# Second attention of a four-layer kernel: global keys laid out as a diagonal, scaling on ScalarE, later counts, global values in two parts

## What is computed

```python
s_loc = jnp.einsum('blhd,blwhd->bhlw', Q, Kw) * scale
a_loc = jax.nn.softmax(s_loc, axis=-1)
local = jnp.einsum('bhlw,blwhd->blhd', a_loc, Vw)
Kg = K[:, global_indices]
Vg = V[:, global_indices]
s_g = jnp.einsum('blhd,bghd->bhlg', Q, Kg) * scale
a_g = jax.nn.softmax(s_g, axis=-1)
glob = jnp.einsum('bhlg,bghd->blhd', a_g, Vg)
out = 0.7 * local + 0.3 * glob
x = layernorm(x + (out.reshape(Bb, Ll, Dm) @ Wo.T + bo))
```

## Time and profile before

| what | us |
|---|---|
| median of 3 runs | 1109.08 (1107.51 to 1109.56) |
| the profiled execution | 1103.31 |
| its span, first to last instruction | 1101.6 |
| PE busy | 953.2 (87%) |
| DVE busy | 781.5 (71%) |
| POOL busy | 678.9 (62%) |
| ACT busy | 577.6 (52%) |

### The profile page before, as it was taken

How to read it: one execution, slowest core, us unless ns; L and a number is a source line. 1 busy time by engine, 2 the same in 40 slices (tenths; PEclk the granted TensorE clock), 3 DMA queues, 4 the chain that set the end, 5 groups by cost and what they waited for, 6 DMA issues and landing times.

```text
span 1101.6 us, 27734 instructions
## 1 busy us (share of the span) xinstructions
PE 953.2 (87%) x7536; PEld 699.0 (63%) x7536; DVE 781.5 (71%) x3615; ACT 577.6 (52%) x1250; POOL 678.9 (62%) x1491
## 2 busy tenths in 40 slices
PE   3999999999959995799999999999999319999940
PEld 1777777777735552677777777777776218777830
DVE  3788888888825776457786877777775327888846
ACT  2566676666621332255555555555545007777734
POOL 3566666666631322266769888887879523777765
PEclk9899999999978998599999999999989559999975
DMA  6121111211042441111112121212211166777717
GB/s 184 27 52 32 45 45 31 48 27 45 23 132 91 161 164 80 32 47 34 47 29 59 39 59 48 68 44 60 53 32 38 44 173 234 238 234 250 254 58 212
DMA packets 71375, 98.34 MB, mean 89 GB/s; under 512 B 13688, under 2 KB 43256, under 8 KB 71104
## 3 DMA queue, kind: packets, MB, share of 16 engines
q1 hardware_dynamic: 61040, 83.31, 25.9%
q0 software_dynamic: 4992, 10.30, 2.8%
q10 hardware_dynamic: 5232, 3.42, 1.2%
HBM read 49.48 MB, written 24.77 MB: 67 GB/s over the span
## 4 chain that ended last, share of the span: by engine, by line
PE 73%; DVE 10%; issue 5%; DMA 3%; POOL 3%; ACT 2%; SPq 2%; DVEq 0%; ACTq 0%; POOLq 0%
PE bank L342 6%; PE bank L172 5%; PE bank L253 5%; PE bank L351 4%; PE bank L372 4%; PE bank L1491 4%; PE bank L1492 4%; PE bank L1257 4%; PE bank L1493 4%; PE bank L406 4%; PE bank L168 3%; PE bank L413 3%; PE bank L346 3%; PE bank L381 3%; PE bank L398 2%
## 5 line engine op out<-in xcount | busy, mean ns | idle before, releaser
L528 ACT ACTIVATE p<-bank 128x480 f32<-128x480 f32 (+1 forms) x448 | 240.5, 540 | 247.8 <-PE bank L372 88.0
L663 DVE CUSTOM_DVE_ANT_0 bank<-bank,band 128x160 f32<-128x160 f32 x512 | 156.9, 347 | 82.0 <-PE bank L342 79.5
L663 DVE CUSTOM_DVE_ANT_0 bank<-bank,causal 128x128 f32<-128x128 f32 (+1 forms) x512 | 169.4, 386 | 56.1 <-PE bank L346 40.3
L893 POOL TENSOR_SCALAR_AFFINE_SELECT p<-p 128x380 f32<-128x380 f32 (+1 forms) x256 | 146.5, 602 | 57.2 <-ACT p L528 56.2
L1669 POOL DMA_INDIRECT y_rows<-p,rows x92 | 105.9, 1151 | 67.5 <-DVE p L1622 46.2
L663 DVE DVE_READ_ACCUMULATOR2_ANT nm<- 128x1 f32 x1024 | 143.6, 140 | 0.1
L874 POOL TENSOR_SCALAR_AFFINE_SELECT p<-p 128x256 f32<-128x256 f32 (+1 forms) x192 | 91.0, 486 | 68.3 <-ACT p L528 64.6
L342 PE MATMUL bank<-ks,qs 128*128 128x186 f32 x512 | 118.6, 316 | 3.5 <-issue 2.3
L342 PEld LDWEIGHTS bank<-ks,qs 128*128 128x128 f32 x512 | 81.5, 198 | 38.2 <-issue 23.3
L372 PE MATMUL bank<-qs,ks 128*128 128x160 f32 x512 | 102.2, 303 | 0.0
L1562 ACT ACTIVATE p<-bank,wb 128x512 f32<-128x512 f32 x92 | 63.6, 691 | 39.5 <-PE bank L1493 37.6
(11 more groups left out here) (207 smaller groups left out, 2330.0 us busy)
## 6 DMA issues: line engine op xcount, KB each, us to landing
qs<-parts SPq DMA_DIRECT2D x46, 512.0 KB, 5.2
qs<-qf SPq DMA_DIRECT2D x128, 128.0 KB, 2.4
rows<-xr SPq DMA_DIRECT2D x23, 260.0 KB, 3.7
parts<-ks SPq DMA_DIRECT2D x8, 512.0 KB, 2.8
xs<-x_b SPq DMA_DIRECT2D x16, 256.0 KB, 4.0
p<-in_w SPq DMA_DIRECT2D x12, 256.0 KB, 3.4
xin<-in_x SPq DMA_DIRECT2D x16, 128.0 KB, 2.2
parts<-qf SPq DMA_DIRECT2D x4, 512.0 KB, 2.7
```

The source lines that it names most:

```text
L528: act.activation(pb[:, :, :].rearrange("p u c -> p (u c)")[:, lo:lo + cols], bank[:, 0:cols], ACT.Exp, scale=SCALE).then_inc(L.exp_done, 1)
L663: return dve.tensor_tensor_reduce(at, at, mask, -1.0, -BIG, ALU.add, ALU.min, nm[:, item:item + 1])
L893: pool.affine_select(out=at, in_=at, compare_op=ALU.is_ge, fill=0.0, base=base, pattern=[[0, 4], [sign, hi - lo]], channel_multiplier=-sig ...
```

## The change

- The global keys are laid out by DVE as a diagonal (`lay_out_kg`, 128 x 400 elements, at (1,2)): one full-width matmul for each four heads takes the place of four narrow ones, so that unit 3 exists in quarters 2 and 3 alone, with two f32r matmuls of 256 columns and one exponential over 512 columns each. They read the unspread queries, kept in three buffers (`T.qf`), to which SP sends the maxima's rows as well.
- The global values are multiplied by `global_values` in two parts, at (3,1) and at (0,1), with the exponentials as the stationary operand: four f32 matmuls of 64 columns each, straight into the turned form that `normalise` reads. Part 2 of `pv`, `round_og` and the copy L479 are gone.
- Scaling (`layernorm`) of the local attention is done by ACT at the end of the body; POOL makes the shift for it with two more small operations.
- `round_rp` and `round_rt` stand at (1,1), the sums on DVE and POOL's sends half a batch later.
- A bank of `normalise` is free when the operation that reads it is done (`rden`), not at the end of the whole.
- `round_kg` stands at the end of the body, followed by two matmuls into a bank that nobody reads (`keep_array_busy`); the next `pass1` waits for the first of `keep_kg`'s two operations.

The core of the diff:

```diff
-ROUNDS = (("pj0", "og", "mx0", "ont", "mx1", "y", "q1", "xt", "mx3"),
-          ("rp", "ot", "pj1", "rt", "q0", "vg", "rl", "mx2", "k0", "k1", "kg"))
+ROUNDS = (("pj0", "mx0", "ont", "mx1", "y", "q1", "xt", "mx3"),
+          ("ot", "pj1", "rp", "rt", "q0", "vg", "rl", "mx2", "k0", "k1", "kg"))
...
-            "ot": (L.on_done, k - 1), "og": (L.on_done, k - 1), "ont": (L.ot_kept, k - 1), "y": (L.r_done, k - 1),
+            "ot": (L.rden, 4 * (k - 2) + 3) if L.local else (L.on_done, k - 1), "ont": (L.ot_kept, k - 1), "y": (L.r_done, k - 1),
...
+        def global_values(pair):
+            batch, par = (fin, p) if pair else (i - 1, n)
+            pe.wait_ge(L.exp_done, L.unit2(batch + 1, 2 + pair, 3) + 1)
+            if pair == 0:
+                pe.wait_ge(L.vg_kept, batch + 1)
+                wait(pe, L.on_done, batch)
             for tau in range(2):
+                out = T.og[:, tau * S:(tau + 1) * S].rearrange("p (r t z) -> p r t z", r=2, t=4)
+                for t in (2 * pair, 2 * pair + 1):
+                    m = pe.matmul(out[:, :, t, :], T.pg[pair][:, t % 2 * S + tau * P:t % 2 * S + (tau + 1) * P],
+                                  T.vgb[par][:, t, :].rearrange("p (r z) -> p r z", r=2),
+                                  start=tau == 0 and t == 0, stop=True, skip_group_check=True)
...
             if L.local and u == 3:
-                for t in range(4):
-                    m = pe.matmul(bank[32 * t:32 * t + 32, 0:S], T.kg[par][:, t, :], q[:, t, :].bitcast(F32),
-                                  start=True, stop=True)
+                pe.wait_ge(L.kd_done, i)
+                for c in range(2):
+                    t = 2 * (j - 2) + c
+                    m = pe.matmul(bank[:, c * S:(c + 1) * S], T.kg[n][:, t, :], T.qf[(i - 1) % 3][:, t, :],
+                                  start=c == 0, stop=True, skip_group_check=True)
...
+        def lay_out_kg():
+            dve.tensor_tensor(T.kg[p].rearrange("p t (j g) -> p t j g", j=4)[:, :, :, 0:NG], keys, mask,
+                              ALU.mult).then_inc(L.kd_done, 1)
...
+        def layernorm():
+            act.wait_ge(L.rstd, L.deviation_steps * (fin + 1))
+            for tau in range(2):
+                act.activation(W.x_next[:, 2 * fin + tau:2 * fin + tau + 1, :], T.r[:, tau:tau + 1, :], ACT.Identity,
+                               scale=T.rs2[:, tau:tau + 1], bias=T.shift[:, tau:tau + 1]).then_inc(L.x_out, 1)
```

250 lines of the change are left out of this document (142 added, 108 removed).

## The result

The changed kernel is slower: median 1124.3 us of four runs (1121.8 to 1129.1) against 1108.3 us for the kernel before, ratio 1.016, 95% interval 1.011 to 1.022. A second set of runs on another occasion gave 1.026 (1.016 to 1.036). The forecast was 1105.4 us, range 1097 to 1112. Both its sign and its range were wrong.

A forecast was written before the change was run, and what follows sets the result against it. PE was taken as the bound (49.4 of 50 us busy), with the DVE and POOL ring binding after the change. Terms 2.5 - 3.0 - 1.3 - 1.3 - 0.6 = -3.7 us took 1109.1 to 1105.4 us, range 1097.0 to 1112.0.

The forecast's parts named there:

- PE's own sum: PE, one iteration of the second attention: 4.04 us gone less 0.76, 1.80 and 0.49 added, 0.99 less.
- The wait at (1,1): PE at pass1 of (1,1) waits for DVE's maxima until S+7.8 (S: iteration's start), 0.8 us, replacing L604's wait.
- The ring: Chain from normalise on DVE through maxima, POOL's quarters 1 and 2 and the residual to pass1 of (3,1), at S+19.23.
- Where the ring binds: At pass1 of (3,1), PE ready at S+18.84 waits for maxima until S+19.23; period 24.78 us.
- What a wait costs: PE's waits at (1,1) and (3,1), some 0.8 and 0.5 us, counted at their length; clock 1.00 expected in steady stretch.
- rival (d): Clock falls as before at iteration 15, for the new waits of 0.8 and 0.5 us: 2 us back, 1107.4 us; 9%.
- The terms for this stretch: Iterations 5 to 14: ten times +0.25 us is +2.5; the stall in front of iteration 15 gone, -1.3.
- Rival (c): Diagonal's layout on DVE holds up POOL's quarter 1: +0.9 instead of +0.25 us an iteration, 1112 us; 15%.
- The head: Before POOL sends: -0.4 us each in iterations 2 to 4, -1.0 in 1, -0.8 at the head; together -3.0.
- The stall in front of iteration 15 and the part behind it: Stall removed by scaling on ACT, -1.3 us; POOL's earlier start from iteration 15, -1.3; last iterations, -0.6.

The follow-up runs named there:

- fill: Changed kernel plus four idle identity matmuls in front of the turning of queries at the end of quarter 2: 1110.7 us, 1.003 of the kernel before.
- gv_late: Changed kernel with the second part of the global values behind the third pass1 of quarter 0 instead of ahead: 1110.6 us, 1.006 of the kernel before.
- kg_q3: Changed kernel with the layout of the diagonal of global keys moved from quarter 1 to quarter 3: 1109.1 us, 1.003 of the kernel before.
- all3_tail: Kernel with three moves plus 10 or 12 idle matmuls in front of PE's waits in iterations 15 to 17: 1078.7 us, 0.982 of the kernel before.
- xb0_fill: Changed kernel with POOL's residual-and-bias sum in quarter 0 and two idle matmuls before the turning of queries: 1107.7 us, 1.001 of the kernel before.
- before_ln_act: Kernel before with only the layernorm scaling moved from DVE to ACT, and POOL's two shift operations: 1106.0 us, 1.003 of the kernel before.
- xb0_gv: Changed kernel with two moves: residual-and-bias sum in quarter 0, second part of global values behind the third pass1: 1082.5 us, 0.980 of the kernel before.
- all3: Changed kernel with three moves: residual-and-bias sum in quarter 0, global values' second part behind third pass1, key layout in quarter 3: 1085.0 us, 0.985.

## Why the prediction was wrong, point by point

- **PE's own sum, -0.99 an iteration.** Right within 0.3. In the changed kernel a unit of two matmuls of 256 columns is 609.53 - 609.24 = 0.29 us (I took 0.38), a part of the global values 0.92 (0.90), and the idle matmuls with the wait for the keys 610.96 - 610.35 = 0.61 (0.49). With these the sum is 4.04 - 0.58 - 1.84 - 0.61 = 1.01, and L604's wait is another 0.2. With three moves the period fell by 1.5; the last 0.3 I haven't followed.
- **The wait at (1,1), 0.8 us at S+7.8.** Measured 0.60, ending at S+7.62. POOL's quarter 1 begins at 593.77 = S+7.84, where S+8.05 was given; the residual at S+17.3, where it was 8.05 + 9.13 = S+17.2. The ring was read correctly up to there.
- **Where the ring binds.** This step failed first. I looked for the next wait at `pass1` of (3,1), for the maxima. PE meets the residual one operation earlier, at the turning of queries, because their bank was last read by it; the list of rounds by bank, `ROUNDS`, says so, and I looked at it for the operations that moved, not for the next one behind. By the prediction's own terms PE would have been there at 18.19 - 0.20 - 0.36 - 3 x 0.92 + 0.29 + 0.90 + 0.8 = S+16.86 (measured 16.90), and the residual would have ended at S+17.6: 0.8 us of waiting, and nothing at (3,1). The period would hardly have changed by that (25.0), but the wait would have been named at 0.8 to 1.3 us instead of 0.4.
- **What a wait costs.** This step cost the sign, and it is the step that failed by the most: the sum has no term for a lower clock in iterations 5 to 14. I priced waits at their own length, and the fall of the clock only at iteration 15 (rival (d), 2 us). With about 2 us of waiting in 25, one wait of them over 1 us, the clock went to 1.2 GHz in five places, each worth some 5 us (274.9 - 250.0 over five). The terms for this stretch, +2.5 and -1.3 for the stall at its end, were right at a full clock: together +1.2, and `fill` has 250.0 - 248.2 = +1.8. They lacked 25 us. The Trainium skill, page "TensorE: Matmul & The Clock Gate", section "A second HAM failure mode: psum-queue depth-cycling", says that a PE that is idle for short moments between groups of matmuls can swing between its two clocks. By that page, which I didn't weigh, this was a rival that ends slower; this case's traces agree, with the five falls of the changed kernel behind waits of 1.0 to 1.3 us at a PE that is busy 92% of an iteration. They also have such waits without a fall (five in a row in `gv_late`).
- **Rival (c), the layout holds up POOL.** Of all the times given, 1112 was the nearest, still 12 us short, and its cause was not the one: the masks lost 0.37 us an iteration, not 0.66, and at a full clock the period was 0.37 longer by it (iteration 6 took 25.03 us with it and 24.66 in `kg_q3`), 3.7 us in ten iterations.
- **The head, -3.0.** Measured -6.4: -0.6 in iteration 0 (I had -0.8), another -0.8 ahead of it, where I had nothing, some -0.65 in each of iterations 2 to 4 (I had -0.4), and 3.1 in iteration 1, 23.05 to 19.97 (I had -1.0). There the kernel before had 3.4 us at 1.2 GHz, from 472.3 us on, which I had not looked for. How much of the 3.1 us is that stretch isn't shown.
- **The stall in front of iteration 15 and the part behind it, -3.2.** The stall is gone as forecast. But from iteration 15 on the changed kernel takes 5.4 us more, not 1.9 less: PE has long waits there (1.57 us at (1,1)), and the granted clock of the first 45 us is 0.77 on average:

```profile
836.38:881.38 45.00, 38.73 (x303) 30.75 (x302) 22.03 (x123) 17.37 (x39) 33.50 (x79) 0.77 0.09 28
```

  In the kernel before it is 0.92 in the first 42 us. That a shorter PE stretch leaves more idle time in a part that others bound, and so a lower clock, is my reading: in `all3_tail` the filled waits hold the clock and this part is 4 us shorter in the one profiled execution, but the medians don't confirm it.

## What to carry to other kernels

When a change gives time back on a PE that was busy all the time, ask first where the slack collects: if it collects in waits that add up to one or two microseconds in each round, the clock may take back more than was gained (here 25 us in ten rounds, in a change forecast to give 3.7). Follow each bank to the operation that last read it, not only each value to who made it, and move what the late operation waits for (here one sum on POOL) to a place where its engine is idle. A handful of matmuls without use, put in the wait, is a quick test of whether a loss is clock or ring. Repeat it on more than one variant: the same waits of 0.6 and 0.2 us went with no fall in `fill` and with two in `xb0_fill`.

## What was not expected of the hardware

- PE, busy 92% of an iteration at 2.4 GHz, fell to 1.2 GHz behind waits of 1.02 to 1.32 us, in `before_ln_act` behind one of 0.89, in `kg_q3` at the end of one of 0.79, and six times in four other variants within 3 us behind one of 0.6. In `fill`, with waits of 0.6 and 0.2 us in each of iterations 5 to 14, it never fell, and `gv_late` bore five waits of 1.0 to 1.3 us in a row, `xb0_gv` one of 1.4. With waits of at most 0.4 us in these iterations (`all3`) it never fell.
- 0.37 us less on POOL in an iteration made 15 us of 1124, and one operation of 0.74 us moved made 21.
- A DVE operation of two SBUF operands and 400 elements took between 0.57 and 2.60 us, according to whether POOL's masks ran beside it.
